# Local attention's softmax sums by four 32x32 matmuls instead of one 128x128, with the orders planned anew

## The reference

```python
patches = extract_patches(x)                        # 25 shifted copies of x
p = patches.reshape(N, NHEADS, hdim, K2, H, W)      # K2 = 25, hdim = 8
q = x.reshape(N, NHEADS, hdim, 1, H, W)
scores = (p * q).sum(axis=2, keepdims=True)
att = jax.nn.softmax(scores, axis=3)                # over the 25 shifts
out = (p * att).sum(axis=3).reshape(N, D, H, W)
out = jnp.einsum('ndhw,od->nohw', out, w_out) + b_out[None, :, None, None]
```

## Time and profile before

| | |
|---|---|
| median of 3 runs | 1961.32 us (1961.11 to 1963.88) |
| the profiled execution, its own time | 1962.19 us |
| span of its trace | 1960.4 us |
| mean granted TensorE clock | 0.897 |
| busy share of the span | PE 79%, DVE 83%, ACT 53%, POOL 59% |
| seven periods from one map's maximum to the next | 121.8, 123.8, 126.3, 120.0, 123.7, 125.6, 119.7 us |

### The profile page before, as it was taken

How to read it: one execution, slowest core, us unless ns; L and a number is a source line. 1 busy time by engine, 2 the same in 40 slices (tenths; PEclk the granted TensorE clock), 3 DMA queues, 4 the chain that set the end, 5 groups by cost and what they waited for, 6 DMA issues and landing times.

```text
span 1960.4 us, 53519 instructions
## 1 busy us (share of the span) xinstructions
PE 1557.5 (79%) x21545; PEld 789.1 (40%) x21545; DVE 1627.2 (83%) x2105; ACT 1044.7 (53%) x1927; POOL 1162.3 (59%) x843
## 2 busy tenths in 40 slices
PE   5889999999999999244986949859598595994935
PEld 3667777777777777100221212212122121221413
DVE  5987777777777777479999999899999999999724
ACT  3566677766777666234455554554645545444200
POOL 4434544444545445004869969698796987964800
PEclk9999999999999999675997969969799697996968
DMA  6000000000000000422014140141401404005069
GB/s 266 1 1 33 4 29 33 0 33 0 33 0 33 0 41 14 115 52 52 2 45 112 29 114 16 43 113 28 111 20 43 113 25 113 21 14 223 23 231 401
DMA packets 46596, 126.42 MB, mean 64 GB/s; under 512 B 12644, under 2 KB 24932, under 8 KB 41316
## 3 DMA queue, kind: packets, MB, share of 16 engines
q1 hardware_dynamic: 46436, 124.04, 20.5%
HBM read 79.04 MB, written 38.54 MB: 60 GB/s over the span
## 4 chain that ended last, share of the span: by engine, by line
PE 51%; DVE 28%; issue 10%; ACT 5%; SPq 2%; DMA 1%; DVEq 1%; POOLq 0%; POOL 0%; ACTq 0%
PE PS L1380 11%; PE PS L1267 8%; DVE PS L1140 7%; PE PS L1357 7%; DVE arena L1159 6%; PE PS L1255 6%; PE PS L1343 5%; PE PS L1221 4%; PE PS L1246 3%; DVE consts L1101 3%; DVE arena L1148 2%; PE PS L1400 2%; DVE arena L1053 2%; DVE arena L1134 2%; PE PS L1225 2%
## 5 line engine op out<-in xcount | busy, mean ns | idle before, releaser
L777 POOL TENSOR_TENSOR arena<-arena 128x1856 f32<-128x1856 f32 (+8 forms) x182 | 670.8, 3726 | 237.5 <-ACT arena L911 188.5
L1159 DVE TENSOR_TENSOR arena<-arena,PS 128x1568 f32<-128x1568 f32 x382 | 658.9, 1781 | 26.8 <-PE PS L1380 25.2
L1343 PE MATMUL PS<-arena,consts 128*32 128x285 f32 (+10 forms) x2176 | 252.6, 540 | 197.8 <-POOL arena L777 128.0
L1380 PE MATMUL PS<-arena,consts 32*32 32x392 f32 x12800 | 385.3, 511 | 22.8 <-DVE arena L1159 22.3
L735 POOL TENSOR_TENSOR arena<-arena,consts 128x196 f32<-128x196 f32 x512 | 294.2, 609 | 161.5 <-ACT arena L825 157.0
L953 ACT ACTIVATE PS<-arena 128x392 f32<-128x392 f32 x382 | 190.9, 501 | 344.2 <-DVE arena L1159 342.3
L1267 PE MATMUL PS<-arena 128*128 128x96 f32 x2048 | 265.7, 273 | 3.1 <-ACT arena L838 1.6
L1267 PEld LDWEIGHTS PS<-arena 128*128 128x128 f32 x2048 | 249.9, 192 | 5.3 <-issue 3.5
L1357 PE MATMUL PS<-arena,consts 128*128 128x392 f32 x400 | 193.2, 578 | 52.2 <-DVE arena L1148 52.2
L742 POOL TENSOR_TENSOR arena<-arena 128x392 f32 (+1 forms) x64 | 78.6, 1228 | 255.2 <-DVE arena L1080 255.2
L1343 PEld LDWEIGHTS PS<-arena,consts 128*32 128x32 f32 x2176 | 50.3, 115 | 396.0 <-issue 182.2
(11 more groups left out here) (97 smaller groups left out, 1663.1 us busy)
## 6 DMA issues: line engine op xcount, KB each, us to landing
arena<-x_dram SPq DMA_DIRECT2D x32, 616.0 KB, 7.5
arena<-x_dram SPq DMA_DIRECT2D x240, 77.0 KB, 2.0
arena<-in_x_dram SPq DMA_DIRECT2D x8, 1568.0 KB, 14.7
x_dram<-arena SPq DMA_DIRECT2D x8, 1568.0 KB, 5.2
attn_dram<-arena SPq DMA_DIRECT2D x256, 49.0 KB, 1.9
arena<-x_dram SPq DMA_DIRECT2D x8, 1568.0 KB, 17.6
arena<-attn_dram SPq DMA_DIRECT2D x8, 1568.0 KB, 17.6
out_dram<-arena SPq DMA_DIRECT2D x8, 1568.0 KB, 24.7
```

Source lines behind the costliest of these rows:

```text
L777: nc.gpsimd.tensor_tensor(tile, x_part, by, ALU.mult).then_inc(pool_tile, 1)
L1159: nc.vector.tensor_tensor(by_channel(v_tiles[n % V_RING]), shifted_values(half, k), over_channels(PS[:, 2 + n % W_BANKS, 0:PIX]), ALU.mult ...
L1343: mm = nc.tensor.matmul(PS[g * GROUP:(g + 1) * GROUP, 0, 0:(hi - lo) * cols], fold, tile[:, (g * rows + lo) * cols:(g * rows + hi) * cols] ...
L1380: mm = nc.tensor.matmul(PS[dst, 4 + i, 0:PIX], ident[src, src], tile[src, c * PIX:(c + 1) * PIX], start=done == 0, stop=done == NK - 1)
```

## The change

Each total, one matmul of the 128x128 identity with all 128 partitions of the exponentials, becomes four matmuls of 32x32 pieces of the identity: rows 0 to 31 with rows 0 to 31, and so on along the diagonal, into the same places of `lsum`. The planner's assumed time of a total goes from 0.72 to 0.32, and the orders of PE and ACT follow from it; the hand-written orders of DVE and POOL do not depend on it, and SP's list comes out the same.

```diff
-            add("pe", ("total", j, k), 0.72, [("exp", j, k // KS), ("sub", j, SUB_PARTS - 1), ("total", j, k - 1) if k else None])
+            add("pe", ("total", j, k), 0.32, [("exp", j, k // KS), ("sub", j, SUB_PARTS - 1), ("total", j, k - 1) if k else None])
...
-                mm = nc.tensor.matmul(lsum, ident, sc[j % 2][:, k, :], start=k == 0, stop=k == NK - 1)
+                for i in range(GROUPS):
+                    rows = slice(i * GROUP, (i + 1) * GROUP)
+                    mm = nc.tensor.matmul(lsum[rows], ident[rows, rows], sc[j % 2][rows, k, :],
+                                          start=k == 0, stop=k == NK - 1)
                 if k == NK - 1:
                     mm.then_inc(total_done, 1)
```

## The result

| | before | after |
|---|---|---|
| median | 1961.4 us (1961.1 to 1963.9, 4 runs) | 2005.7 us (2004.7 to 2006.9, 4 runs) |
| span of the profiled execution | 1960.4 us | 2004.0 us |
| mean granted TensorE clock | 0.897 | 0.898 |

What follows compares the result with a forecast made beforehand. DVE was taken as the bound, with PE counting only through DVE's stops: 8.8 + 10.4 + 3.8 + 12.1 - 1.6 - 2.2 = +31.3 us on 1961.3 gave 1992.6, say 1993. Own range 1978 to 2010; whole range 1957 to 2042.

Steps and rivals of the forecast that it cites:

- (b): First half of maps 0 to 6: PE's blocks of value sums and totals fall behind DVE's products; +10.4 us.
- (a): Start of maps 0 to 6: added totals ahead of the first value sum make DVE wait longer; +8.8 us.
- (c): Middle of maps 0 to 6: the weight of product 27 now waits behind the eviction on ACT; +3.8 us.
- rival 1: Small totals really cost a quarter, 0.22 us, so the new order fits and is faster: 1942.5 us; chance 0.17.
- rival 2: Dearer blocks: each total costs a full 0.88 us, about +78 us in all, 2040 us; chance 0.12.
- rival 3: PE's high clock returns later after the first small total of a map: 2007 us; chance 0.09.
- (d): Ahead of the next maximum, maps 0 to 6: last score copy behind eviction and mostly two pixel steps; +12.1 us.
- (e): The reciprocal's waits go, because a map's last total comes 24 products early; -1.6 us.
- (f): Map 7: half 1 has no totals, so pairs of products shorten, and the reciprocal's wait goes; -2.2 us.
- Stop at V3: Sign at a map's start: DVE stops 1.5 to 3 us there, for the first value sum behind four totals.
- V T V at 1.55 or less: Sign in PE's timeline, first half: value sum, total, value sum at 1.55 us or less, not 1.73.
- Rival 4: Nearly nothing: 0.68 us holds for totals and value sums, half of (a) and (d) goes, 1970 us; chance 0.12.

Runs made afterwards that it cites:

- weight_first: The changed kernel with the weight of product 27 put back ahead of the eviction of half 0 on ACT; 1995.2 us, ratio 1.0159 against before.

## Why the prediction was right, and where it was not

**The verdict and its reason held.** Slower, by the orders and not by the shape: the kernel with the shape alone is the faster one, and that with the order alone the slowest. The planner's new lists are as the prediction wrote them. 2005.7 lies in the forecast's own range, 1978 to 2010, 13 us above the point. That it came this near is in part luck: (b) was 15 us too low, and (a) and (c), 3.7 and 2.5 too high, made up for some of it.

**The cost of a total.** Taken: 0.68 inside a block, 0.80 as its last unit after one value sum. Measured: 0.66 and 0.80. That was read from two score sums in a row, of another shape and by columns, and it held. But 0.66 is no gain of the small shape as such: a large total behind a large one adds the same. A total as a quarter of the old one (rival 1) would have been some 0.22: the runs show 0.06 saved a total in V T V, and rival 1 is out. The Trainium skill's "Up to 4×" (TensorEngine Tiling (Array Packing), Theoretical Speedup) is not what this replacement gives; no run here shows more than 0.24 saved of 0.85. The other rule cited, the Trainium skill's TensorE: Matmul & The Clock Gate (Part 3), that a packed group spans one matmul's duration, fits the 0.66 inside a long block, close to the 0.68 that streaming 392 columns was estimated at.

**(b), the mis-sized term.** Forecast +10.4, measured +25.7. The formula for a block of n was 0.88 + 0.68 (n - 1) + 0.12. Measured, for blocks of three to five with two or three value sums in which totals stand between them, it is 0.88 + 0.66 (n - 1) + 0.34. What was wrong is the 0.68 for the second value sum of a block. With one value sum the formula is right: V T 1.68 for 1.68, V T T 2.35 for 2.36. The second value sum costs 0.86 behind a total and 1.00 behind a value sum; the third, in V T V T V, 0.66. In the count of the prediction, three blocks of three, seven of four, one of five, one V T and eleven score sums: 7.6 + 22.4 + 3.9 + 1.7 + 10.0 = 45.6 for the forecast 43.7, so 4.8 us late a map, 33 in seven (measured 34.9) and +24 over before. (The 1.6 that the prediction put for V23 T23 is 1.68 by its own formula, which changes nothing.) What mixed blocks of the small shape cost was in no row of before, but there was a bound: three value sums in a row took 0.91 each, which the prediction named and used only for rival 2. Rival 2 itself, 0.88 for each unit, is out: in V T V T V the fourth and fifth cost 0.66.

**(a)** Forecast +8.8, measured +5.1. The added total cost little where the clock returned meanwhile:

```profile
1190.16 4.61 PE L1359 MATMUL PS<-arena,consts 32*32 32x392 f32 x32 [4.00 <-DVE arena L1148]
1194.70 0.89 PE L1343 MATMUL PS<-arena,consts 128*32 128x406 f32 x8
```

Four small totals take 4.54 where three large ones took 4.21; the 5.6 of the low clock throughout did not come. Busy time in two short stretches there (the clock is the third number from the end):

```profile
1190.10:1193.50 3.40, 3.34 (x24) 1.04 (x28) 3.40 (x4) 2.66 (x4) 3.40 (x2) 0.50 0.46 112
1193.90:1196.00 2.10, 2.10 (x52) 0.63 (x45) 1.30 (x1) 0.64 (x2) 0.29 (x1) 1.00 0.43 112
```

The clock rises about 3.6 us after the first total; over the eight maps this was 2.8 to 6.0 us in after and 1.8 to 6.0 in before. Small totals do not bring the high clock later: rival 3 is out. The four maps with one more total behind T T T lost 0.2 us together and not 3.0, and part of that is where the clock happened to rise: 3.5, 6.0, 5.4 and 4.7 us after the first total before the change, 3.0, 3.6, 4.1 and 4.3 in after. In weight_first, which has the same list on PE, it rose after 5.2, 2.8, 5.8 and 3.2, and DVE stood 2.3, 1.1, 2.6 and 1.3 us in these maps; (a) was 14.1 there for the 12.4 of after. Map 0, and the two maps that had no stop, got 1.5, 1.6 and 1.9 of the forecast 1.4, 2.2 and 2.2.

**(c)** Forecast +3.8, measured +1.3. The stop went to V27 as forecast, 1.31 us and not 1.8 to 2.0; putting the weight first took 6.5 us away, which shows the place and the mechanism.

**(d)** Forecast +12.1, measured +13.2, stop by stop 4.39, 5.20, 5.35, 5.15, 5.14, 5.17 and 3.57 for the forecast 3.6, five times 5.1 (which is 25.5 and not the 25.7 that it added), and 3.6. Undoing the one move on ACT took 13.7 of it back.

**(e), (f).** Reciprocal -1.6 as forecast, map 7 -2.5 for -2.2.

**The signs named in advance.** Stop at V3: 1.1 to 2.3 where 1.5 to 3 was said. Products of the first half: 1.93 each (1.70 + 34.9/7/22), said 1.80 or more. A stop at V27, none at V28: so. L1140's idle 37.3, said near 36, released by L938. No wait of L1166. Only V T V at 1.55 or less failed: within a block the two instruction streams interleave and no start to start can be read; by blocks a V T pair ahead of another V is 2.54 - 0.88 = 1.66. At 1.66 it lies half-way between the forecast's sign and rival 2's 1.75, as the error in (b) does.

**Rival 4** (half of (a) and (d) vanishes) is out by (d). What hid the rest, POOL, held: it is not among the releasers of DVE in the table of waits.

**Open**: why the second value sum of a block costs 0.86 or 1.00 and the third, in V T V T V, 0.66. That needs a kernel in which only the number of matmuls of a value sum changes; it wasn't tried. Open too are the single waits behind (c) and (d) when lists of two plans are mixed.

## What to carry to other kernels

Where an order is planned from assumed costs, a wrong cost does harm through the order, not through the operation: a total assumed at 0.32 that costs 0.66 to 0.80 turned a kernel that the edit itself made 0.55% faster into one 2.2% slower. Change the operation and the plan in two steps, and put the measured cost of the step in its surroundings into the planner. When a timeline shows stops of the bound engine after every second step, add up one period of the engine that never pauses, whichever engine the releaser's name points to.

## What the runs showed of the hardware that was not expected

- The records of a total and of the next value sum interleave. In the timeline of after above, the value sum begins at 1081.18, the total's first four instructions at 1081.86, the next value sum's first four at 1082.12 and the total's next one at 1082.19. So matmuls of neighbouring steps overlap, and their records do not even start in the order in which the program lists the steps; a step has a cost only as part of its block. A value sum works on all 16 32x32 places and a total on four of them; which place a record belongs to the trace does not say.
- What a unit adds depends on what stands ahead of it: in V T V T V 0.88, 0.80, 0.86, 0.66 and 0.66 with small totals, a steady 0.85 to 0.88 with large ones. A total right behind a total adds 0.66, and that with the large one too. Two value sums side by side are dearest: the second adds 1.00.
- The same change of shape was worth, by the ratios, 0.55% (order of before), 0.7% (totals three places later), 1.0% (order planned anew) and 1.45% (totals spread evenly), or 11, 13, 20 and 28 us: its worth is set by the blocks that the totals stand in and by how much of the map DVE waits for PE, not by the operation alone.
